# A fused attention and mixture-of-experts kernel: 64x64 state blocks, the router's logits on their own, and a new order of the steps

## What is computed

```python
x = x + conv(_ln_c(x))                      # conv: linear causal attention, 8 heads of 16
t = tokens(x)
t = t + ffn(_ln_t(t))                       # ffn: 8 experts, top 2, 128 -> 128
# conv
q, k, v = Wq x + bq, Wkv x + bkv            # per position, 128 -> 128 each
Q, K = elu(q) + 1, elu(k) + 1
den = 1 / (sum_d(Q * cumsum_over_heads(K)) + 1e-10)
S_t = S_(t-1) + K_t (outer) V_t ; num_t = Q_t S_t      # a running state, per head 16x16
out = num * den
# ffn
logits = xf @ gate_w + router_gamma ; probs = softmax(logits) ; top-2 weights
out = sum_e combine_e * (gamma * (xf @ expert_w_e + expert_b_e) + beta_e)
```

## Time and profile before

| | us |
|---|---|
| median of 3 runs | 755.08 (754.4 to 756.46) |
| the profiled execution, its own time | 755.91 |
| its span, first to last instruction | 754.1 |
| PE busy | 717.1 (95%) |
| DVE busy | 685.9 (91%) |
| ACT busy | 409.9 (54%) |
| POOL busy | 397.8 (53%) |
| mean granted TensorE clock | 0.982 of full |

### The profile page before, as it was taken

One profiled execution on the slowest core, in us unless ns is written; L12 is line 12 of the kernel. 1 busy time (PEld: TensorE's weight loads), 2 busy tenths in 40 slices (PEclk: granted clock), 3 DMA queues, 4 the chain that ended last, 5 costly groups with the idle time before them and its releaser, 6 DMA issues.

```text
span 754.1 us, 23195 instructions
## 1 busy us (share of the span) xinstructions
PE 717.1 (95%) x8137; PEld 624.0 (83%) x8137; DVE 685.9 (91%) x2550; ACT 409.9 (54%) x1261; POOL 397.8 (53%) x639
## 2 busy tenths in 40 slices
PE   4767999999999999999999999999999999999986
PEld 2666888888888888888888888888888888888875
DVE  4567999999999999999999999999999999999984
ACT  1122666655555666666665555555555555555544
POOL 5145555555555555555555555555555555555520
PEclk9769999999999999999999999999999999999999
DMA  5101111111111111111111111111111111111101
GB/s 129 33 15 30 42 40 35 37 40 37 39 37 42 42 42 42 42 42 42 42 42 42 42 42 42 42 42 42 42 42 42 42 42 42 42 30 29 30 16 29
DMA packets 60214, 30.29 MB, mean 40 GB/s; under 512 B 2160, under 2 KB 60176, under 8 KB 60176
## 3 DMA queue, kind: packets, MB, share of 16 engines
q1 hardware_dynamic: 60176, 29.79, 14.4%
HBM read 20.34 MB, written 9.44 MB: 39 GB/s over the span
## 4 chain that ended last, share of the span: by engine, by line
PE 91%; DVE 4%; POOL 2%; ACT 1%; issue 1%; DMA 1%; SPq 0%; DVEq 0%; ACTq 0%; POOLq 0%
PE bank L877 11%; PE bank L915 10%; PE bank L894 9%; PE bank L916 9%; PE bank L917 9%; PE bank L933 8%; PE bank L901 4%; PE bank L909 4%; PE bank L884 4%; PE bank L853 3%; PE bank L854 3%; PE bank L855 3%; PE bank L860 3%; PE bank L847 2%; PE bank L866 2%; PE bank L935 2%
## 5 line engine op out<-in xcount | busy, mean ns | idle before, releaser
L574 DVE TENSOR_TENSOR probs<-bank,tri 128x512 f32<-128x512 f32 x288 | 184.9, 684 | 10.2 <-PE bank L877 4.7
L397 ACT ACTIVATE y_act<-bank,scale 128x128 f32<-128x128 f32 x576 | 159.4, 383 | 2.5
L915 PE MATMUL bank<-e_high,x_high 128*128 128x512 f32 x288 | 124.0, 431 | 1.1 <-DVE o L803 1.1
L916 PE MATMUL bank<-e_low,x_high 128*128 128x512 f32 x288 | 113.7, 395 | 0.0
L917 PE MATMUL bank<-e_high,x_low 128*128 128x512 f32 x288 | 113.5, 394 | 0.0
L311 POOL TENSOR_TENSOR qn<-feat,rden 128x512 f32<-128x512 f32 x36 | 38.2, 1061 | 116.4 <-DVE rden L672 116.4
L416 ACT ACTIVATE x_high<-x 128x512 fp32r<-128x512 f32 x36 | 22.8, 633 | 137.0 <-DVE x L664 137.0
L592 DVE SCALAR_TENSOR_TENSOR y_dve<-bank,scale,y_dve 128x128 f32<-128x128 f32 x288 | 92.4, 343 | 0.0
L580 DVE SCALAR_TENSOR_TENSOR qkv<-bank,rstd,b_qkv 128x384 f32<-128x384 f32 x144 | 86.8, 605 | 5.1 <-POOL rstd L301 2.6
L387 ACT ACTIVATE k_odd<-bank,parity 128x512 f32<-128x512 f32 x36 | 24.7, 687 | 114.4 <-PE bank L860 114.4
L933 PE MATMUL bank<-ident,y_act 128*128 128x128 f32 x576 | 80.8, 273 | 1.6 <-ACT y_act L397 1.6
(11 more groups left out here) (139 smaller groups left out, 1764.5 us busy)
## 6 DMA issues: line engine op xcount, KB each, us to landing
x<-in_x SPq DMA_DIRECT2D x36, 256.0 KB, 3.3
x_res<-in_x SPq DMA_DIRECT2D x36, 256.0 KB, 3.2
out<-o SPq DMA_DIRECT2D x36, 256.0 KB, 2.4
beta_raw<-in_L_ffn_beta_w SPq DMA_DIRECT2D x1, 512.0 KB
e_raw<-in_L_ffn_expert_w SPq DMA_DIRECT2D x1, 512.0 KB
w_raw<-in_L_conv_Wkv SPq DMA_DIRECT2D x2, 64.0 KB, 2.4
b_qkv<-in_L_conv_bkv SPq DMA_DIRECT2D x1, 128.0 KB, 4.4
w_raw<-in_L_conv_Wq SPq DMA_DIRECT2D x1, 64.0 KB, 2.6
```

The source lines that it names most:

```text
L397: last = nc.scalar.activation(y_act[:, p, u, e], bank[EXPERTS_AT[u][0]][:, 128 * e:128 * e + 128], ACT.Copy, scale=scale[:, p, u, e:e + 1])
L574: return tt(probs[:, half, i].rearrange("p u e t -> p (u e) t"), bank[SCORES_AT[half][i]][:].rearrange("p (n t) -> p n t", t=T), tri[:].un ...
L915: mm(out, x1_high[:, p, u], e_high[:, w], start=True, stop=False)
L916: mm(out, x1_high[:, p, u], e_low[:, w], start=False, stop=False)
```

## The change

- `key_values`: for each image two products of 64x64 (keys 64i to 64i+63 by values 64i to 64i+63) at two column positions of the PE array, in place of one 128x128 product. `kv_new` and `state` become 64 wide, and DVE's mask is `pair_mask`, made once from `heads_mask`.
- `from_state`: for each image two products with 64x64 weights on the array's diagonal (rows and columns 64i to 64i+63), in place of one with 128x128.
- `turn_x1` becomes four plain transposes into one bank; a new function `logits` multiplies x1 by the 8 router columns (4 fp32 products, weights 128x128, 8 columns). ACT copies the logits in one piece.
- `turn_y` takes two images at a time, alternating between them.
- `LAGS` is 7: turn_x and x's statistics are now at g[2], projections at g[3], attention at g[4] and g[5], experts at g[6]; g[0] holds only the load of x, g[1] nothing. turn_k stands in the same step as its projections, and keys are copied by ACT a step later.
- The order on every engine and the PSUM banks are new.

```diff
-AT = dict(x=4, kv=3, att=6, x1_a=6, x1_b=4, k=1, q=7, coef=0, out=1)
+AT = dict(x=1, kv=0, att=5, x1_a=6, x1_b=6, k=2, q=5, coef=3, out=1)
-LAGS = 6
+LAGS = 7
-        kv_new = sb("kv_new", [128, U, 128])
-        state = sb("state", [128, IMAGES, 128])
+        pair_mask = sb("pair_mask", [128, 64])
+        kv_new = sb("kv_new", [128, U, 64])
+        state = sb("state", [128, IMAGES, 64])
...
+                tt(pair_mask[:], heads_mask[:, 0:64], heads_mask[:, 64:128], ALU.add).then_inc(S["first_dve"], 1)
...
-                    tt(kv_new[:], bank[AT["kv"]][:].rearrange("p (u d) -> p u d", u=U),
-                       heads_mask[:].unsqueeze(1).broadcast_to([128, U, 128]), ALU.mult)\
+                    tt(kv_new[:], bank[AT["kv"]][:, 0:64 * U].rearrange("p (u d) -> p u d", u=U),
+                       pair_mask[:].unsqueeze(1).broadcast_to([128, U, 64]), ALU.mult)\
...
-                    last = mm(bank[AT["att"]][:, T * u:T * u + T], state[:, U * p + u], q_t[:, p, u],
-                              start=(u == 0), stop=False, skip_group_check=True)
+                    for i in range(2):
+                        rows = slice(64 * i, 64 * i + 64)
+                        last = mm(bank[AT["att"]][rows, T * u:T * u + T], state[rows, U * p + u], q_t[rows, p, u],
+                                  start=(u == 0), stop=False, skip_group_check=True)
...
-                    last = mm(bank[AT["kv"]][:, 128 * u:128 * u + 128], feat[:, p, u, 128:256], qkv[:, p, u, 256:384],
-                              start=True, stop=True)
+                    for i in range(2):
+                        last = mm(bank[AT["kv"]][64 * i:64 * i + 64, 64 * u:64 * u + 64],
+                                  feat[:, p, u, 128 + 64 * i:128 + 64 * i + 64],
+                                  qkv[:, p, u, 256 + 64 * i:256 + 64 * i + 64], start=True, stop=True)
...
-                    out = bank[AT["x1_a"]][:, WIDE * u:WIDE * (u + 1)] if u < IN_N else bank[AT["x1_b"]][:, 0:WIDE]
-                    last = mm(out, x1[:, p, u], id_gate[:], start=True, stop=True)
+                    last = transpose(bank[AT["x1_a"]][:, T * u:T * u + T], x1[:, p, u], ident[:])
+            def logits(p):
+                for u in range(U):
+                    last = mm(bank[AT["x1_b"]][:, EXPERTS * u:EXPERTS * u + EXPERTS], x1[:, p, u], id_gate[:, T:WIDE],
+                              start=True, stop=True)
...
-            def turn_y(p, u):
-                for e in range(4):
-                    mm(out, y_act[:, p, u, e], ident[:], start=False, stop=False, is_transpose=True,
+            def turn_y(p, half):
+                for e in range(5):
+                    for u in (2 * half, 2 * half + 1):
+                        last = mm(bank[AT["out"]][:, T * u:T * u + T], y_act[:, p, u, e] if e < 4 else y_dve[:, p, u],
+                                  ident[:], start=False, stop=(e == 4), is_transpose=True, skip_group_check=True)
```

More of the change, by code:

```diff
@@ new lines, in step @@
+                if g[6]:
+                    n, p = g[6].i, g[6].par
+                    need(dve, "hot_ab", n + 1)
+                    tt(coef[:, p], probs_e[:, 0], hot[:, 2], ALU.mult).then_inc(S["coef"], 1)
+                    need(dve, "soft_scaled", n + 1)
+                    tt(scale[:, p], probs_e[:, 1], hot[:, 2], ALU.mult).then_inc(S["scale"], 1)
+                if g[5]:
+                    n, p = g[5].i, g[5].par
+                    need(dve, "values_1", n + 1)
+                    need(dve, "values_0", n + 1)
+                    dve.wait_ge(x_res_loaded[p], 16 * (g[5].half + 1))
+                    need(dve, "out", n - 1)
+                    tt(flat(x1, p), bank[AT["att"]][:], flat(x_res, p), ALU.add).then_inc(S["x1"], 1)
@@ new lines, in step @@
+                if g[6]:
+                    n, p = g[6].i, g[6].par
+                    need(dve, "y_one_2", n + 1)
+                    weigh(p, 2, 0).then_inc(S["y_dve_20"], 1)
+                    need(dve, "y_dve_11", n + 1)
+                    weigh(p, 1, 2).then_inc(S["y_dve_12"], 1)
+                    need(dve, "y_dve_20", n + 1)
+                    weigh(p, 2, 1).then_inc(S["y_dve_21"], 1)
+                if g[2]:
+                    n = g[2].i
+                    need(dve, "x_turned", n + 1)
+                    parts([bank[AT["x"]][:, T * u:T * u + T] for u in range(U)], bn).then_inc(S["x_parts"], 1)
@@ L879, in scores @@
                 return last
-            def from_state(p):
-                for u in range(U):
-                    last = mm(bank[AT["att"]][:, T * u:T * u + T], state[:, U * p + u], q_t[:, p, u],
-                              start=(u == 0), stop=False, skip_group_check=True)
-                return last
             def values(p, half):
@@ L969, in step @@
[L969 to L975 removed]
+                    need(pe, "x_low", n + 1)
+                    need(pe, "k_even", n)
+                    need(pe, "k_odd", n)
+                    project(p, 0).then_inc(S["proj_0"], 1)
+                    need(pe, "probs_02", n - 1)
@@ L989, in step @@
                     values(p, 0).then_inc(S["values_0"], 1)
+                if g[6]:
+                    n, p = g[6].i, g[6].par
+                    need(pe, "out", n)
+                    if k is not None:
+                        need(pe, "x_parts", n + 4)
+                    experts(p, 0, 0).then_inc(S["experts_00"], 1)
+                    need(pe, "probs_00", n + 2)
+                    if k is not None:
+                        need(pe, "y_one_0", n)
+                        need(pe, "y_dve_02", n)
+                    experts(p, 0, 1).then_inc(S["experts_01"], 1)
@@ new lines, in step @@
+                if g[6]:
+                    n, p = g[6].i, g[6].par
+                    need(pe, "qkv_3", n + 4)
+                    if k is not None:
+                        need(pe, "probs_12", n + 2)
+                        need(pe, "y_one_3", n)
+                        need(pe, "y_dve_32", n)
+                    experts(p, 3, 1).then_inc(S["experts_31"], 1)
+                    need(pe, "coef_low", n + 1)
+                    need(pe, "y_act_3", n + 1)
+                    if k is not None:
+                        need(pe, "qkv_1", n + 4)
+                    turn_coef(p).then_inc(S["coef_turned"], 1)
@@ new lines, in step @@
+                    turn_k(p).then_inc(S["k_turned"], 1)
+                if g[4]:
+                    n, p = g[4].i, g[4].par
+                    need(pe, "probs_11", n + 1)
+                    need(pe, "probs_10", n + 1)
+                    need(pe, "kv_new", n + 1)
+                    if k is not None:
+                        need(pe, "lg_raw_a", n)
+                        need(pe, "qkv_2", n + 2)
+                        need(pe, "qkv_1", n + 2)
+                    scores(p, 0).then_inc(S["scores_0"], 1)
+                    if k is not None:
+                        need(pe, "q_t", n + 1)
+                    from_state(p).then_inc(S["from_state"], 1)
```

720 lines of the change are left out of this document (322 added, 398 removed), and 15 rows, old and new, of the table names.

## The result

| | before | after |
|---|---|---|
| median of 4 runs each, same chip | 755.77 (754.4 to 757.15) | 765.44 (763.42 to 767.12) |
| ratio, 95% interval | | 1.013 (1.0108 to 1.0152) |
| profiled execution, its span | 755.91, 754.1 | 763.42, 761.7 |
| first `out` starts | 89.74 | 87.40 |
| the 30 steps behind it, each | 19.22 | 19.62 |

The change makes the kernel 1.3% slower; the forecast was 2.0%. The span grew by 7.6 us: -2.3 before the first `out`, 30 x 0.40 = +12.0 in the loop, -2.0 in the last five intervals.

The account below looks back on a forecast made before the run. PE's instruction stream was taken to bound the loop, 19.21 us a step. Terms +0.41 - 0.43 + 0 + 0.54 = +0.52 a step; 33 x 0.52 = +17.2, less 2, gives +15: median 770 us, range 752 to 782.

Parts of the forecast that it names:

- The logits: PE, x1 and logits: joint product -0.93, four transposes +0.44, 8 new records +0.90; together +0.41 us a step.
- B: Logits' weights load behind neighbouring transposes, 8 columns cost what 64 would: 0.46, so +0.08 a step, 755.7 us; chance 0.12.
- C: Both cheap logits and free ends of part-array sections: step -0.46, 738 us, faster; chance 0.07.
- key_values: PE, key_values: 8 overlapping pairs cost 0.46 instead of 0.89, -0.43 a step; two ends of its own add +0.34.
- A: Blocks 64 wide enter without a price at their ends: step -0.02, 752.4 us; chance 0.10.
- E: The column positions of key_values don't overlap: +0.43 a step, 784 us; chance 0.03.
- from_state: PE, from_state: diagonal blocks overlap, so body change 0; one more end than before beside scores 0, +0.20 a step.
- rival D: The diagonal blocks of from_state don't overlap: +0.89 a step, 799 us; chance 0.10.
- The rest keep theirs: PE, ends of the other part-array sections (`values` 2, `scores` 1 and `scores` 0): their cost stays unchanged.
- The number of steps and the end: 35 steps, the last few holding less: 33 x 0.52 = +17.2 us; the last steps get shorter as before.
- The start: Before the first `out`: weights come some 3 us sooner; -2 us in all, between -5 and +3.
- The other engines: kv_new some 0.3 less, POOL's `state` halved, one ACT logits copy; DVE's room from 0.7 to 1.5 us, counted at nothing.

Follow-up runs that it names:

- 128x128 blocks: The changed kernel with key_values, kv_new, `state` and from_state back at 128x128, order and all else kept: 766.74 us, 1.014 of before.
- joint product: The changed kernel with x1's transposes and logits again one product with `id_gate`, turn_q and ACT's logits copy moved to suit: 769.39 us, 1.016 of before.
- x1_low later: The changed kernel with POOL's x1_low (1.28 us) moved behind the last two sums of k_sum: 765.61 us, 1.012 of before.

## Why the forecast was right, and where it was off

*PE's stream sets the step*: right. PE is busy 384 of 384 us in after, and where PE was full and its rows were taken apart, the step moved by what they say, to within 0.04 us.

*The logits*: +0.41 forecast, +0.36 in after (0.85 for the 8 records, not 0.90), +0.41 in the kernel with that edit alone. The choice that decided it, the row with the same weights and one column, was the right neighbour: the number of columns plays no part from 8 to 64. (Before's clock rows begin at 21.3 us, at the full clock, so the row at 21.37 ran at the full rate, as assumed; the half rate ahead of it is read from the spacings alone.) That was the point on which rivals B and C stood, and they fall.

*key_values*: body -0.43 forecast and measured; its ends +0.34 forecast, 0.35 measured in after, 0.30 in before's order. Rivals A and E fall.

*from_state*: the diagonal blocks overlap, so rival D falls; the shared end +0.20 forecast, +0.17 measured.

*"The rest keep theirs"* was wrong by 0.06: the second scores' ends got cheaper when key_values left their side. The sum of the step's terms was +0.52 and should have been +0.40: 0.05 from the logits, 0.06 from this, 0.03 from from_state, less 0.02 for key_values and rounding.

*The number of steps and the end*: I took 33 steps' worth of the difference, "35 steps of which the last few hold less", and no gain in the last ones. The 30 steps behind the first `out` carry it, and the last five intervals together are 2.0 us shorter than before, not longer. This is the second step that failed, worth 3 x 0.40 + 2.0 = 3.2 us. Together with 33 x 0.12 = 4.0 for the size of a step, and 0.3 at the start, it makes up the miss: 15 forecast, 7.6 in the spans. Why the last intervals are shorter stays open, but one piece of it comes with the new order and not with the blocks: the last interval but one is 15.5 to 15.9 us in all four kernels that have this order (after, 128x128 blocks, joint product, x1_low later), 17.7 in before and 17.1 to 18.1 in the others. The five together vary even so, from 82.2 to 84.1 among the four, and no run took that apart.

*The start*: -2 forecast, -2.3 measured, but this is no proof of the reason. The weights' products did start at 12.81 instead of 15.94 and turn_k at 33.03 instead of 33.80. Among the 14 profiles the first `out` lies between 87.40 and 91.05, and two kernels whose edits don't touch the start lie near both ends (87.72 with the logits apart, 90.97 with key_values in 64x64 blocks). The granted clock between 20 and 60 us differs from profile to profile (from 20 to 40 us 0.74 in before, 0.59 in after, 0.91 with the 128x128 blocks).

*The other engines*: kv_new fell from 692 to 411 ns as expected, but DVE's room shrank to 0.65 instead of growing to 1.5, through the stretch of lg2. In after it cost nothing. Had both the logits and the ends been cheap, as rival C had it, DVE's 18.96 would have stood in the way of a step of 18.75. PE waits nowhere in after's loop, as forecast. Of DVE's three waits of about 0.5 one is there, for turn_x (0.44).

## What to carry to other kernels

Where PE's stream is full, cost a change of its products by the spacing of the starts, per weight load and per column, and count the ends where products on part of the array meet products on the whole of it: here 0.28 to 0.43 us for a section with both ends of its own, about half of that where a neighbour with another part form shares one, and none where the neighbour has the same form. Splitting a product so that the same weights are loaded twice costs the load again, however few columns the second has; making blocks smaller paid where the columns shrank too (key_values), and not where only the weights did (from_state). And before moving work to where its ends are shared, look at which engine's lateness it covers: the same blocks brought 4 us behind `values`, 9 between bias and turn_y, and 17 between scores and bias.

## What the runs showed of the hardware that I had not expected

A small DVE operation whose inputs both lie in SBUF is held until a POOL operation beside it ends: 182 ns became 1143 ns in the mean (128x32 beside POOL's 128x512, 1.28 us), while `probs`, which reads one input from PSUM and starts within POOL's qk as `rank` does, keeps its 0.66 (443.99, above). It happens where an order puts them side by side, and so a reordering changes DVE's load without changing its work. By the Trainium skill, SBUF — State Buffer, "SBUF: two separate sides", DVE with two SBUF inputs and a GpSimd operation that reads SBUF take one pair of ports in turn, the one that starts first holding it for its whole instruction. Both traces agree: lg2 in after starts 0.16 behind POOL's operation and ends 0.04 behind its end, and so does `rank` in the other trace, 0.70 behind its start and 0.04 behind its end.

The ends of part-array sections depend on the neighbour: 32-row scores and 32-column key_values side by side save one change (-0.15 a step), and key_values behind `values`, both with weights of 128x32, has no end between them. By the Trainium skill, TensorEngine Tiling (Array Packing), Key Properties, each change of the mode drains the engine, a change of the tile alone doesn't. The traces agree: 0.22 us from the last set of scores to the first of key_values, 0.11 from the last set of `values` to the first of key_values. That the time lost is a drain, no row shows.
